# Where the right-hand score units of a sequence block stand in the step loop of a fused attention, LayerNorm and FFN kernel

## The chip, the cores and the metric

The kernel runs on the 8 cores of one Trainium2 chip. Every core computes two of the sixteen sequences with the same program, and no core waits for another. The metric is the device time of the slowest core in microseconds (us).

## The reference

```python
def attn(x):                                  # x: (16, 2048, 1024)
    q = (x @ Wq + bq); k = (x @ Wk + bk); v = (x @ Wv + bv)   # 16 query heads of 64, 2 kv heads
    # position s sees the 256 positions s-128 .. s+127 (keys and values padded with zeros)
    scores = jnp.einsum('bgrsd,bgswd->bgrsw', qg, k_win)
    probs = jax.nn.softmax(scores, axis=-1)
    out = jnp.einsum('bgrsw,bgswd->bgrsd', probs, v_win)
    return out @ Wo + bo
x = layernorm(x + attn(x))
x = layernorm(x + ffn(x))                     # ffn: complex 512 x 512 linear map, W from two small factors
```

## The kernel before, in words

The two sequences of a core are worked through one after the other (variable b). A sequence has 16 blocks of 128 positions. `emit_qkv(b, q)` loads four blocks of x, casts them to bf16 (ACT, L371), transposes them (PE, L381) and makes the queries QT, the keys KT and the values VB of a group of four blocks. Groups 0 and 1 are made ahead of the step loop, groups 2 and 3 at the end of steps 5 and 9.

The step loop has 18 steps k. Step k works on three blocks at once: S = k (scores), P = k-1 (attention, output projection, first LayerNorm) and Q2 = k-2 (FFN, second LayerNorm). The units are:

- `sc_unit(b, S, c, pair)`: two score matmuls (L509) of block S against key block S-1+c, c = 0, 1, 2, into two of the three PSUM banks pSC. The banks go round, (2u)%3 and (2u+1)%3 for the unit with the running number u, so the first matmul of a unit needs the second exp of the unit two before it, and the second matmul needs the first exp of the unit just before it.
- `exp_unit`: the two exps of that unit on ACT (L527), from pSC to EX. The first waits until both matmuls of the unit are done. `mask_unit`: the two masks on GpSimd (POOL, L541) for c = 0 (maskl) and c = 2 (maskr).
- `av_unit(b, P, quad)`, quad = 0 to 3: twelve matmuls (L564) of the masked EX tiles of all three c with VB into pAV[quad % 2]. It waits until that bank has been read by `normts_unit` of quad - 2. `recip_unit` (L582) and `normts_unit` (L592, four instructions) on DVE read the bank.
- `attnT_unit`: eight transposes (L614) and a copy on DVE (L622). `wo_unit`: nine matmuls for each half of the output projection (L639, L643) into pW[0] and pW[1]. `ln1_unit` on DVE: two adds (L682), the sum of squares (L652, tile scr) and four small steps. `rstd1_unit` on ACT: L699 and L704, which wait for the last small step. `x1norm_unit` on DVE (L717).
- `x1t_unit`: eight transposes (L737) and a copy (L744). `ffn_unit`: nine matmuls for each half (L766, L770) into pW[0] and pW[1]. `ln2out_unit`: two adds (L785), which free pW, the same sum of squares (L652), L798 and L803 on ACT, L811 on DVE and the store of y from POOL's queue (L819).

There is no scheduler. Each engine runs its instructions in the order in which the units are called, and a wait on a semaphore holds up everything behind it on its engine. Across engines the order is free but for those waits.

```python
            banks = ((2 * u) % 3, (2 * u + 1) % 3)
                    E.wait(E.res(f"pSC{banks[gq]}")["f"])
                E.wait(E.res(f"avb{quad % 2}")["f"])
                E.wait(E.ev[f"var1_{ring}"])
```

Of the kernel before, what the change touches and what calls it, by code (L numbers as in the profile page):

```python
# [18 lines left out]
def build_nc(debug=False):  # L19
# [138 lines left out]
    def schedule(E):  # L158
# [374 lines left out]
        def mask_unit(b, S, c, pair):  # L533
            m = maskl if c == 0 else maskr
            for gq in range(2):
                quad = pair * 2 + gq
                exi = (S % 2) * 12 + c * 4 + quad
                ev_e = E.ev[f"exp_{S % 2}_{c}_{quad}"]
                if cur == "g":
                    E.wait(ev_e)  # L540
                i = gps.tensor_mul(EX[:, exi * 512:(exi + 1) * 512],  # L541
                                   EX[:, exi * 512:(exi + 1) * 512], m[:]) \
                    if cur == "g" else None
                E.ev[f"msk_{S % 2}_{c}_{quad}"] = E.inc("g", i)

        def av_unit(b, S, quad):
            g = quad % 2
            bank = quad % 2
            vready = E.res(f"VB{S // 4}")["r"]
            vnext = E.res(f"VB{min(S // 4 + 1, 3)}")["r"]  # L550
            if cur == "t":
                E.wait(E.res(f"avb{quad % 2}")["f"])
                E.wait(vready)
                E.wait(vnext)
                for c in range(3):
                    key = ("msk" if c != 1 else "exp") + f"_{S % 2}_{c}_{quad}"
                    E.wait(E.ev[key])
            first = True
            i = None
            for c in range(3):  # L560
                kb = S - 1 + c
                exi = (S % 2) * 12 + c * 4 + quad
                for hh in range(4):
                    i = ten.matmul(  # L564
                        pAV[bank][:, hh * 65:(hh + 1) * 65],
                        EX[:, exi * 512 + hh * 128: exi * 512 + (hh + 1) * 128],
                        VB[:, (kb + 1) * 130 + g * 65: (kb + 1) * 130 + (g + 1) * 65],
                        start=first, stop=(c == 2 and hh == 3)) if cur == "t" else None
                    first = False
            ev = E.inc("t", i if cur == "t" else None)  # L570
            E.ev[f"av_{S % 2}_{quad}"] = ev
            for c in range(3):
                E.res(f"exfree{(S % 2) * 12 + c * 4 + quad}")["f"] = ev

        def recip_unit(b, S, quad):
            ring = S % 2
            i = None
            if cur == "v":
                E.wait(E.ev[f"av_{S % 2}_{quad}"])
                if quad == 0:  # L580
                    E.wait(E.res(f"attn{ring}")["f"])
                i = vec.reciprocal(Rrec[:, ring * 16 + quad * 4: ring * 16 + (quad + 1) * 4],  # L582
                                   ap3(pAV[quad % 2], 64, [[512, 128], [65, 4]]))
            E.inc("v", i)
# [252 lines left out]
        for b in range(NB):  # L837
            if b > 0:
                E.res("KTfree")["f"] = E.ev["lastAV"]["f"]
                E.res("VBfree")["f"] = E.ev["lastAV"]["f"]  # L840
            emit_qkv(b, 0)
            emit_qkv(b, 1)
            if b == 0:
                emit_wbuild()
            if debug and b == 0:
                if cur == "g":
                    gps.wait_ge(SEMH["s"], E.res("QT1")["r"][1])
                    gps.dma_start(dbg["dqt"], QT[:]).then_inc(SEMH["dc"], 16)
                E.c["dc"] += 16
            for k in range(18):  # L850
                S, P, Q2 = k, k - 1, k - 2
                if S < 16:
                    sc_unit(b, S, 0, 0)
                    exp_unit(b, S, 0, 0)
                if 0 <= P < 16:
                    av_unit(b, P, 0)
                if S < 16:
                    sc_unit(b, S, 0, 1)
                    exp_unit(b, S, 0, 1)
                    mask_unit(b, S, 0, 0)  # L860
                    mask_unit(b, S, 0, 1)
                if 0 <= P < 16:
                    av_unit(b, P, 1)
                if 0 <= Q2 < 16:
                    x1t_unit(b, Q2)
                    ffn_unit(b, Q2, 0)
                if 0 <= P < 16:
                    recip_unit(b, P, 0)
                    recip_unit(b, P, 1)
                    normts_unit(b, P, 0)  # L870
                    normts_unit(b, P, 1)
                if S < 16:
                    sc_unit(b, S, 1, 0)
                    exp_unit(b, S, 1, 0)
                if 0 <= P < 16:
                    av_unit(b, P, 2)
                if 0 <= Q2 < 16:
                    ffn_unit(b, Q2, 1)
                if S < 16:
                    sc_unit(b, S, 1, 1)  # L880
                    exp_unit(b, S, 1, 1)
                if 0 <= P < 16:
                    av_unit(b, P, 3)
                    recip_unit(b, P, 2)
                    recip_unit(b, P, 3)
                    normts_unit(b, P, 2)
                    normts_unit(b, P, 3)
                    attnT_unit(b, P)
                if S < 16:
                    sc_unit(b, S, 2, 0)  # L890
                    exp_unit(b, S, 2, 0)
                    mask_unit(b, S, 2, 0)
                if 0 <= Q2 < 16:
                    ln2out_unit(b, Q2)
                if 0 <= P < 16:
                    wo_unit(b, P, 0)
                if S < 16:
                    sc_unit(b, S, 2, 1)
                    exp_unit(b, S, 2, 1)
                    mask_unit(b, S, 2, 1)  # L900
                if 0 <= P < 16:
                    wo_unit(b, P, 1)
                    ln1_unit(b, P)
                    rstd1_unit(b, P)
                    x1norm_unit(b, P)
                if k == 5:
                    emit_qkv(b, 2)
                if k == 9:
                    emit_qkv(b, 3)
                if debug and b == 0 and k == 9:  # L910
                    if cur == "g":
                        gps.wait_ge(SEMH["s"], E.res("KT3")["r"][1])
                        gps.wait_ge(SEMH["v"], E.res("VB3")["r"][1])
                        gps.dma_start(dbg["dkt"], KT[:]).then_inc(SEMH["dc"], 16)
                        gps.dma_start(dbg["dvb"], VB[:]).then_inc(SEMH["dc"], 16)
                    E.c["dc"] += 32
            E.ev["lastAV"] = {"f": ("t", E.c["t"])}
# [88 lines left out]
```

## Time and profile before

| what | us |
|---|---|
| device time, median of 2 runs (1401.92 and 1407.13) | 1404.53 |
| the profiled execution | 1403.19 |
| its span, on the slowest core (4) | 1401.6 |
| spans of the eight cores | 1388.2 to 1401.6 |

The span runs from the first to the last instruction of a core. All durations in this text are from the profiled execution on core 4. The lines L... are those of the kernel before; the functions that the steps call stand above the changed lines and have the same numbers in both kernels.

### The profile page before, as it was taken

The numbers are of one execution on the slowest core, as the hardware profiler recorded it, in microseconds if no ns is written. First come the engines' busy times: TensorE is split into PE (matmuls) and PEld (weight loads), VectorE is DVE, ScalarE is ACT, GpSimd is POOL, SyncE is SP. The second block draws the span as 40 slices with busy tenths as digits, with TensorE's granted clock in tenths as the row PEclk, the third lists the DMA queues.
The fourth block names the chain that finished last, engine by engine and source line by source line (L and its number), as shares of the span: only waits on it lengthen the run. The fifth ranks groups of instructions, "written<-read, shape, count | busy, mean of one in ns | idle before, by whom it ended". The sixth has DMA issues, their size and how long they took to land.

```text
span 1401.6 us, 17008 instructions; the slowest of 8 cores (1388.2 to 1401.6 us)
## 1 busy us (share of the span) xinstructions
PE 851.1 (61%) x4568; PEld 353.4 (25%) x4568; DVE 534.8 (38%) x1539; ACT 396.3 (28%) x673; POOL 358.2 (26%) x324
## 2 busy tenths in 40 slices
PE   0067334676586666676756576676676658676764
PEld 0033001222232223222222232222232223222221
DVE  0001344354414551445554112445225441555453
ACT  3333113223223223323220234323232323323210
POOL 0000004344213440333430105433223421343310
PEclk9998555677687777777776786777687667777676
DMA  4521000000200001000000300000200020000000
GB/s 131 164 78 31 0 0 0 1 25 21 76 0 16 16 33 59 16 16 16 21 26 15 106 31 1 16 16 16 76 1 31 15 76 1 16 21 26 16 16 30
DMA packets 15869, 44.51 MB, mean 32 GB/s; under 512 B 3091, under 2 KB 5539, under 8 KB 15782
## 3 DMA queue, kind: packets, MB, share of 16 engines
q0 software_dynamic: 9216, 33.56, 6.9%
q1 hardware_dynamic: 6566, 9.87, 2.4%
q8 instruction: 45, 0.74, 0.2%
q14 instruction: 42, 0.34, 0.1%
HBM read 26.65 MB, written 16.78 MB: 31 GB/s over the span
## 4 chain that ended last, share of the span: by engine, by line
PE 54%; DVE 19%; issue 10%; DMA 7%; ACT 6%; DVEq 1%; POOL 1%; SPq 0%; ACTq 0%; POOLq 0%
PE pW L766 12%; PE pW L639 12%; PE pW L411 9%; PE pSC L509 4%; PE pAV L564 4%; DVE scr L652 4%; DMA xs<-x 4%; DVE attn L592 4%; PE pT L737 2%; ACT EX L527 2%; PE pW L770 2%; PE pW L643 2%; DVE pre L785 2%; PE pT L614 2%; DVE pre L682 1%
## 5 line engine op out<-in xcount | busy, mean ns | idle before, releaser
L527 ACT ACTIVATE EX<-pSC,expbias 128x512 bf16<-128x512 f32 x384 | 242.7, 683 | 369.6 <-PE pSC L509 368.5
L541 POOL TENSOR_TENSOR EX<-EX,maskr_s 128x512 bf16<-128x512 bf16 x128 | 172.3, 1370 | 333.8 <-ACT EX L527 333.2
L541 POOL TENSOR_TENSOR EX<-EX,maskl_s 128x512 bf16<-128x512 bf16 x128 | 149.6, 1198 | 377.7 <-ACT EX L527 377.7
L639 PE MATMUL pW<-wo_sb,attnT 128*128 128x512 bf16 x512 | 179.8, 514 | 37.0 <-DVE pre L785 35.7
L509 PE MATMUL pSC<-QT,KT 64*128 64x512 bf16 x384 | 111.9, 474 | 109.6 <-ACT EX L527 108.5
L411 PE MATMUL pW<-XT,wq_sb 128*128 128x512 bf16 x512 | 129.2, 420 | 8.9 <-DVE XT L391 8.9
L381 PE MATMUL pT<-identb,x_tm 128*128 128x128 bf16 x256 | 32.0, 304 | 152.7 <-ACT x_tm L371 138.4
L592 DVE TENSOR_SCALAR attn<-pAV,Rrec 128x64 bf16<-128x64 f32 x512 | 110.2, 277 | 14.3 <-DVE attn L592 0.5
L766 PE MATMUL pW<-wrt,x1T 128*128 128x512 bf16 x256 | 92.5, 499 | 36.7 <-DVE Rrec L582 34.5
L652 DVE SCALAR_TENSOR_TENSOR scr<-pre 128x1024 bf16<-128x1024 f32 x64 | 104.5, 1633 | 6.7
L582 DVE RECIPROCAL Rrec<-pAV 128x4 f32<-128x4 f32 x128 | 19.7, 173 | 197.3 <-PE pAV L564 197.3
L639 PEld LDWEIGHTS pW<-wo_sb,attnT 128*128 128x128 bf16 x512 | 57.0, 121 | 142.2 <-issue 123.8
L564 PE MATMUL pAV<-VB,EX 128*128 128x65 bf16 x1536 | 81.5, 211 | 8.0 <-ACT EX L527 3.2
L564 PEld LDWEIGHTS pAV<-VB,EX 128*128 128x128 bf16 x1536 | 65.6, 109 | 47.2 <-issue 47.2
L471 DVE COPY VB<-pT 128x128 bf16<-128x128 bf16 x32 | 7.3, 229 | 182.7 <-PE pT L465 182.7
L420 ACT ACTIVATE QT<-pW,bq_sb 128x512 bf16<-128x512 f32 x64 | 44.0, 687 | 112.3 <-PE pW L411 112.3
L411 PEld LDWEIGHTS pW<-XT,wq_sb 128*128 128x128 bf16 x512 | 53.8, 106 | 82.4 <-issue 33.8
L391 DVE COPY XT<-pT 128x1024 bf16<-128x1024 bf16 x32 | 22.1, 692 | 137.1 <-PE pT L381 137.1
L614 PE MATMUL pT<-identb,attn 128*128 128x128 bf16 x256 | 23.3, 244 | 80.2 <-DVE attn L592 80.2
L509 PEld LDWEIGHTS pSC<-QT,KT 64*128 64x128 bf16 x384 | 23.9, 96 | 169.0 <-issue 164.4
L381 PEld LDWEIGHTS pT<-identb,x_tm 128*128 128x128 bf16 x256 | 24.5, 137 | 159.9 <-issue 159.9
L682 DVE SCALAR_TENSOR_TENSOR pre<-pW,x_tm 128x512 f32<-128x512 f32 x64 | 44.0, 688 | 51.5 <-PE pW L643 51.5
(81 smaller groups left out, 789.5 us busy)
## 6 DMA issues: line engine op xcount, KB each, us to landing
xs<-x POOLq DMA_DIRECT2D x32, 512.0 KB, 4.6
y<-outst POOLq DMA_DIRECT2D x32, 512.0 KB, 3.0
wstage<-wq SPq DMA_DIRECT2D x4, 512.0 KB, 4.5
xs<-wq SPq DMA_DIRECT2D x4, 512.0 KB, 4.6
wstage<-wo SPq DMA_DIRECT2D x4, 512.0 KB, 4.6
xs<-wo SPq DMA_DIRECT2D x4, 512.0 KB, 4.6
wstage<-wk SPq DMA_DIRECT2D x1, 512.0 KB, 4.7
xs<-wv SPq DMA_DIRECT2D x1, 512.0 KB, 4.8
```

Source lines behind the costliest of these rows:

```text
L381: i = ten.transpose(pT[:, c * 128:(c + 1) * 128], x_tm[:, slot * D + c * 128: slot * D + (c + 1) * 128], identb[:]) if cur == "t" else None
L411: i = ten.matmul(pW[bank][:, :], wq_sb[:, c * 1024 + t * 128: c * 1024 + (t + 1) * 128], rhsXT(c), start=(c == 0), stop=(c == 7)) \
L509: i = ten.matmul(pSC[banks[gq]][:, :], lhsT, rhs, start=True, stop=True, tile_position=(rowbase, 0)) if cur == "t" else None
L527: i = sca.activation(EX[:, exi * 512:(exi + 1) * 512], pSC[banks[gq]][:, :], AF.Exp, bias=expbias[:])
L541: i = gps.tensor_mul(EX[:, exi * 512:(exi + 1) * 512], EX[:, exi * 512:(exi + 1) * 512], m[:]) \
L564: i = ten.matmul(pAV[bank][:, hh * 65:(hh + 1) * 65], EX[:, exi * 512 + hh * 128: exi * 512 + (hh + 1) * 128], VB[:, (kb + 1) * 130 + g * ...
L592: i = vec.tensor_scalar(attn[:, ring * 1024 + quadcol[quad] + hh * 64: ring * 1024 + quadcol[quad] + (hh + 1) * 64], ap3(pAV[bank], hh * 6 ...
L614: i = ten.transpose(pT[:, c * 128:(c + 1) * 128], attn[:, ring * 1024 + c * 128: ring * 1024 + (c + 1) * 128], identb[:]) if cur == "t" el ...
L639: ten.matmul(pW[half][:, :], attnT[:, ring * 1024 + c * 128: ring * 1024 + (c + 1) * 128], wo_sb[:, c * 1024 + half * 512: c * 1024 + (hal ...
L652: lambda: vec.scalar_tensor_tensor(scr[:], pre_getter(), 1.0, pre_getter(), ALU.mult, ALU.mult, accum_out=stt[:, c0 + 2:c0 + 3]),
L682: i = vec.scalar_tensor_tensor(pre1[:, ring * 1024 + half * 512: ring * 1024 + (half + 1) * 512], pW[half][:, :], 1.0, x_tm[:, slot * D + ...
L766: ten.matmul(pW[half][:, :], x1T[:, ring * 1024 + c * 128: ring * 1024 + (c + 1) * 128], wsrc[:, wc * 512:(wc + 1) * 512], start=(c == 0), ...
```

## The change

The two units of the right-hand key block, c = 2, with their exps and masks leave the end of the step of their own block and are called at the very start of the next one. They read the same tiles there (QT, KT, EX), and their masks are still ahead of the `av_unit` calls that read them. In a full step the four score pairs c = 2 of P and c = 0 of S are therefore called one behind the other. `av_unit(b, P, 0)` moves behind the first FFN half, `sc_unit(b, S, 1, 0)` stands between it and `av_unit(b, P, 1)`, the first reciprocals and `normts_unit` calls follow that, and `sc_unit(b, S, 1, 1)` stands ahead of `av_unit(b, P, 2)`. No unit is added or left out, and no wait is added or removed by hand.

```diff
--- before.py
+++ after.py
@@ -849,36 +849,41 @@
                 E.c["dc"] += 16
             for k in range(18):
                 S, P, Q2 = k, k - 1, k - 2
+                if 0 <= P < 16:
+                    sc_unit(b, P, 2, 0)
+                    exp_unit(b, P, 2, 0)
+                    mask_unit(b, P, 2, 0)
+                    sc_unit(b, P, 2, 1)
+                    exp_unit(b, P, 2, 1)
+                    mask_unit(b, P, 2, 1)
                 if S < 16:
                     sc_unit(b, S, 0, 0)
                     exp_unit(b, S, 0, 0)
-                if 0 <= P < 16:
-                    av_unit(b, P, 0)
-                if S < 16:
                     sc_unit(b, S, 0, 1)
                     exp_unit(b, S, 0, 1)
                     mask_unit(b, S, 0, 0)
                     mask_unit(b, S, 0, 1)
-                if 0 <= P < 16:
-                    av_unit(b, P, 1)
                 if 0 <= Q2 < 16:
                     x1t_unit(b, Q2)
                     ffn_unit(b, Q2, 0)
                 if 0 <= P < 16:
+                    av_unit(b, P, 0)
+                if S < 16:
+                    sc_unit(b, S, 1, 0)
+                    exp_unit(b, S, 1, 0)
+                if 0 <= P < 16:
+                    av_unit(b, P, 1)
                     recip_unit(b, P, 0)
                     recip_unit(b, P, 1)
                     normts_unit(b, P, 0)
                     normts_unit(b, P, 1)
                 if S < 16:
-                    sc_unit(b, S, 1, 0)
-                    exp_unit(b, S, 1, 0)
+                    sc_unit(b, S, 1, 1)
+                    exp_unit(b, S, 1, 1)
                 if 0 <= P < 16:
                     av_unit(b, P, 2)
                 if 0 <= Q2 < 16:
                     ffn_unit(b, Q2, 1)
-                if S < 16:
-                    sc_unit(b, S, 1, 1)
-                    exp_unit(b, S, 1, 1)
                 if 0 <= P < 16:
                     av_unit(b, P, 3)
                     recip_unit(b, P, 2)
@@ -886,19 +891,10 @@
                     normts_unit(b, P, 2)
                     normts_unit(b, P, 3)
                     attnT_unit(b, P)
-                if S < 16:
-                    sc_unit(b, S, 2, 0)
-                    exp_unit(b, S, 2, 0)
-                    mask_unit(b, S, 2, 0)
                 if 0 <= Q2 < 16:
                     ln2out_unit(b, Q2)
                 if 0 <= P < 16:
                     wo_unit(b, P, 0)
-                if S < 16:
-                    sc_unit(b, S, 2, 1)
-                    exp_unit(b, S, 2, 1)
-                    mask_unit(b, S, 2, 1)
-                if 0 <= P < 16:
                     wo_unit(b, P, 1)
                     ln1_unit(b, P)
                     rstd1_unit(b, P)
```

PE in step 6, which is the first after group 2 of `emit_qkv`. Before, from the step's start to the second FFN half (L509 score pairs, L564 attention times values, L737 transposes, L766 and L770 FFN):

```order
L509 MATMUL pSC<-QT,KT 128x512 x2
L564 MATMUL pAV<-VB,EX 128x65 x12
L509 MATMUL pSC<-QT,KT 128x512 x2
L564 MATMUL pAV<-VB,EX 128x65 x12
L737 MATMUL pT<-identb,x_tm 128x128 x8
L766 MATMUL pW<-wrt,x1T 128x512 x4
L766 MATMUL pW<-witn,x1T 128x512 x4
L770 MATMUL pW<-beta_row,ones_row 128x512
L509 MATMUL pSC<-QT,KT 128x512 x2
L564 MATMUL pAV<-VB,EX 128x65 x12
L766 MATMUL pW<-wit,x1T 128x512 x4
L766 MATMUL pW<-wrt,x1T 128x512 x4
```

The same engine and place in the changed kernel:

```order
L509 MATMUL pSC<-QT,KT 128x512 x8
L737 MATMUL pT<-identb,x_tm 128x128 x8
L766 MATMUL pW<-wrt,x1T 128x512 x4
L766 MATMUL pW<-witn,x1T 128x512 x4
L770 MATMUL pW<-beta_row,ones_row 128x512
L564 MATMUL pAV<-VB,EX 128x65 x12
L509 MATMUL pSC<-QT,KT 128x512 x2
L564 MATMUL pAV<-VB,EX 128x65 x12
L509 MATMUL pSC<-QT,KT 128x512 x2
L564 MATMUL pAV<-VB,EX 128x65 x12
L766 MATMUL pW<-wit,x1T 128x512 x4
L766 MATMUL pW<-wrt,x1T 128x512 x4
```

Two score pairs separated by an attention group have become four pairs (eight matmuls) in a row, and the two attention groups of the start now stand behind the first FFN half.

ACT from the first exp of that step into the next one. Before (L527 exp, L798 and L803 the second LayerNorm, L699 and L704 the first):

```order
L527 ACTIVATE EX<-pSC,expbias 128x512 x10
L798 ACTIVATE st<-st 128x1
L803 ACTIVATE rstd<-st,neghalf 128x1
L527 ACTIVATE EX<-pSC,expbias 128x512 x2
L699 ACTIVATE st<-st 128x1
L704 ACTIVATE rstd<-st,neghalf 128x1
L527 ACTIVATE EX<-pSC,expbias 128x512 x10
```

In the changed kernel:

```order
L527 ACTIVATE EX<-pSC,expbias 128x512 x12
L798 ACTIVATE st<-st 128x1
L803 ACTIVATE rstd<-st,neghalf 128x1
L699 ACTIVATE st<-st 128x1
L704 ACTIVATE rstd<-st,neghalf 128x1
L527 ACTIVATE EX<-pSC,expbias 128x512 x12
L798 ACTIVATE st<-st 128x1
```

The two exps between the two LayerNorms have gone, and all twelve exps of a step stand together, behind the first LayerNorm's two instructions.

POOL around the loads of group 2 at the end of step 5. Before (L541 masks, L819 store of y, L363 loads of x):

```order
L541 TENSOR_TENSOR EX<-EX,maskl_s 128x512 x4
L541 TENSOR_TENSOR EX<-EX,maskr_s 128x512 x2
L819 DMA y<-outst 128x1024
L541 TENSOR_TENSOR EX<-EX,maskr_s 128x512 x2
L363 DMA xs<-x 128x1024 x4
L541 TENSOR_TENSOR EX<-EX,maskl_s 128x512 x4
```

In the changed kernel:

```order
L541 TENSOR_TENSOR EX<-EX,maskr_s 128x512 x4
L541 TENSOR_TENSOR EX<-EX,maskl_s 128x512 x4
L819 DMA y<-outst 128x1024
L363 DMA xs<-x 128x1024 x4
L541 TENSOR_TENSOR EX<-EX,maskr_s 128x512 x4
```

The last masks of the step stood between the store and the loads; now they stand behind the loads.

## Rows read from the trace of the kernel before

**Rows 1.** The page: its span and PE's busy time.

```profile
span 1401.6 us, 17008 instructions; the slowest of 8 cores (1388.2 to 1401.6 us)
...
PE 851.1 (61%) x4568; PEld 353.4 (25%) x4568; DVE 534.8 (38%) x1539; ACT 396.3 (28%) x673; POOL 358.2 (26%) x324
```

**Rows 2.** The page: chain that ended last, by engine.

```profile
PE 54%; DVE 19%; issue 10%; DMA 7%; ACT 6%; DVEq 1%; POOL 1%; SPq 0%; ACTq 0%; POOLq 0%
```

**Rows 3.** Windows: length; busy us (instructions) of PE, PEld, DVE, ACT, POOL; clock; DMA.

```profile
616.10:643.66 27.56, 18.89 (x113) 7.61 (x112) 13.99 (x44) 8.48 (x16) 10.35 (x10) 0.75 0.03 13
229.70:238.80 9.10, 6.83 (x15) 1.24 (x14) 5.46 (x4) 7.18 (x12) 7.56 (x5) 0.50 0.00 0
```

**Rows 4.** Timeline, start of step 13: start us, us, instruction, [idle before].

```profile
643.67 0.39 PE L509 MATMUL pSC<-QT,KT 64*128 64x512 bf16 x2
...
644.72 1.78 DVE L652 SCALAR_TENSOR_TENSOR scr<-pre 128x1024 bf16<-128x1024 f32 x1
...
648.21 1.25 ACT L527 ACTIVATE EX<-pSC,expbias 128x512 bf16<-128x512 f32 x2
...
649.02 0.58 PE L509 MATMUL pSC<-QT,KT 64*128 64x512 bf16 x1 [4.17 <-ACT EX L527]
...
650.33 1.04 PE L737 MATMUL pT<-identb,x_tm 128*128 128x128 bf16 x8
...
652.49 0.58 PE L766 MATMUL pW<-wrt,x1T 128*128 128x512 bf16 x1 [1.12 <-DVE Rrec L582]
```

**Rows 5.** Timeline, rest of step 12.

```profile
628.31 0.39 PE L509 MATMUL pSC<-QT,KT 64*128 64x512 bf16 x2
...
628.63 0.54 PE L564 MATMUL pAV<-VB,EX 128*128 128x65 bf16 x12
...
631.47 0.54 PE L564 MATMUL pAV<-VB,EX 128*128 128x65 bf16 x12
...
632.40 1.83 DVE L592 TENSOR_SCALAR attn<-pAV,Rrec 128x64 bf16<-128x64 f32 x8
...
634.49 0.68 PE L614 MATMUL pT<-identb,attn 128*128 128x128 bf16 x8 [2.48 <-DVE attn L592]
...
636.79 3.57 PE L639 MATMUL pW<-wo_sb,attnT 128*128 128x512 bf16 x8 [1.08 <-DVE pre L785]
...
640.83 0.61 PE L509 MATMUL pSC<-QT,KT 64*128 64x512 bf16 x2
...
641.37 2.05 PE L639 MATMUL pW<-wo_sb,attnT 128*128 128x512 bf16 x8
```

**Rows 6.** Timeline, TensorE in step 0, score pairs alone.

```profile
232.75 1.16 PE L509 MATMUL pSC<-QT,KT 64*128 64x512 bf16 x2 [0.35 <-ACT EX L527]
234.26 1.16 PE L509 MATMUL pSC<-QT,KT 64*128 64x512 bf16 x2 [0.35 <-ACT EX L527]
```

**Rows 7.** Windows, tile scr alone, at the ends of 14 steps.

```profile
257.70:263.00 5.30, 1.23 (x2) 0.98 0.00 0
...
343.00:347.90 4.90, 1.32 (x2) 1.00 0.18 70
...
sum 78.30, DVE 27.57; mean DVE 1.97
```

**Rows 8.** Timeline, end of step 5 and loads of group 2.

```profile
369.95 2.27 POOL L541 TENSOR_TENSOR EX<-EX,maskr_s 128x512 bf16<-128x512 bf16 x2
...
372.15 1.13 POOL L363 DMA_DIRECT2D xs<-x  x2
...
374.81 0.29 ACT L704 ACTIVATE rstd<-st,neghalf 128x1 f32<-128x1 f32 x1
...
377.20 1.04 ACT L371 CAST x_tm<-xs 128x1024 bf16<-128x1024 f32 x1 [2.10 <-DMA xs<-x]
```

**Rows 9.** Timeline, start of step 6.

```profile
411.41 0.53 PE L509 MATMUL pSC<-QT,KT 64*128 64x512 bf16 x2 [0.23 <-issue]
...
414.28 1.04 PE L737 MATMUL pT<-identb,x_tm 128*128 128x128 bf16 x8
```

## The prediction

> **What bounds the kernel now.** I read the page first. The span is 1401.6 us and no engine fills it: TensorE (PE) is busy for 851.1 us, ACT for 396.3 us [rows 1]. The chain that ended last puts 54% on PE, 19% on DVE, 10% on gaps between dependent instructions, 6% on ACT [rows 2]. So the bound is a chain that goes from engine to engine inside each step; a step gets longer where PE comes to a wait with nothing queued in front of it.
>
> The windows view gives one step: step 12 takes 27.56 us, in which PE is busy for 18.89, DVE for 13.99, ACT for 8.48 and POOL for 10.35, at a mean granted clock of 0.75 [rows 3]. ACT and POOL have room; the matter is when their work comes.
>
> Then the timeline. PE's waits in a full step are four. (a) At the start: the second matmul of the second score pair waits 4.17 us for the first exp [rows 4]. ACT has just finished the previous step's first LayerNorm, and behind PE's last output-projection matmul that takes long: the step begins at 643.67, DVE starts the sum of squares at 644.72 (1.05 later), it takes 1.78, the exp starts 1.71 after its end (648.21), the matmul 0.81 after that (649.02). (b) 1.12 us ahead of the first FFN half at 652.49, behind the transposes at 650.33. (c) 2.48 us ahead of the transposes at 634.49, from the eight normalisations. (d) 1.08 us ahead of the output projection at 636.79 [rows 5]. The change touches (a), adds a wait between (b) and (c), and takes filling out of (d).
>
> **The change, part by part.** A "full step" is one of steps 2 to 15 of both sequences, 28 in all; 24 begin behind another step's LayerNorm, 4 (steps 6 and 10) begin behind group 2 or 3 of the QKV part, when ACT is already free.
>
> 1. Start of a step, four score pairs in a row. With three PSUM banks a pair's second matmul needs the first exp of the pair before it. Before, the wait for the first exp came in the second pair; it still does, and only the attention group that stood in it (hidden there) is gone. But now two more pairs follow that ACT paces. What that costs is shown by step 0, where the pairs stand alone: they start 1.51 us apart, 232.75 and 234.26 [rows 6]. Before, from the matmul at 649.02 to the transposes at 650.33 it was 1.31 us [rows 4], one matmul and one attention group. Now it is 2 x 1.51 + 0.55 for the last matmul at 1.2 GHz = 3.57, so +2.26. Nothing hides it: the transposes need L717, which was done in time for them at 650.33 [rows 4], but they stand behind the scores in PE's order. Bounds: ACT cannot take less than the 1.25 us of two exps [rows 4] per pair, so at least 2.5 + 0.4 - 1.31 = +1.6.
>
> 2. The masks leave the sum of squares. Two masks used to run on POOL at the step's end. The sum of squares took 1.97 us on average in 14 windows there, but 1.23 where no mask and no store ran beside it, and 1.32 in one with a store (DMA share 0.18) [rows 7]. Now no mask is called between the centre of one step and the next first exp, so I take 1.28: -0.69 in wait (a). Bounds: -0.74 and 0. The masks' new place costs nothing: the four that the moved attention groups need take 2 x 2.27 us [rows 8] behind the first exp, and ahead of the first of those groups stand three more pairs, the transposes and nine FFN matmuls, some 10 us.
>
> 3. The new wait in the middle. `av_unit(P, 2)` reuses the PSUM bank of `av_unit(P, 0)` and waits for its normalisation, which on DVE stands behind the reciprocal of quad 1. Before, both groups were over long before the first FFN half ended, and from the end of that half (628.31) to the last attention group (631.47) it was 3.16 us [rows 5]. Now, counted from the same point: attention group 0.35 (an estimate, between a pair's 0.32 from 628.31 to 628.63 and the group's own 0.54), score pair 0.32, second attention group starts at 0.67. Normalisation starts 0.93 after a group's start (631.47 to 632.40), its first four of eight take half of 1.83, and PE reacts 0.26 after the end (634.23 to 634.49) [rows 5]: the third group starts at 0.67 + 0.93 + 0.92 + 0.26 = 2.78. From there to the last group it was 2.84 with a pair of 0.32 in it, so 2.52: 5.30. That is +2.1. Of it some 0.7 is the two groups that were free at the start of the step, and 1.4 is waiting, net of the pairs. The last group, the reciprocal, and wait (c) follow as before. Bounds: +0.7 if the wait vanished, +2.6 if everything there ran at 1.2 GHz.
>
> 4. End of a step. The pair ahead of the second output-projection half cost 0.54 (640.83 to 641.37) [rows 5] and is gone: -0.5. The pair behind the transposes stood in wait (d), which DVE's add ends, so it gives nothing. Bounds: -0.54 and 0.
>
> 5. Loads of groups 2 and 3, 4 times. The two masks (2.27 us) stood on POOL ahead of the x loads; the first cast on ACT started at 377.20, 2.1 after LayerNorm at 375.1, waiting for the DMA [rows 8]. Without the masks the loads are issued 2.2 earlier, and LayerNorm ends 0.4 earlier: -2.2 each. Bounds: -2.6 and 0.
>
> Sum. 24 steps x (2.26 - 0.69 + 2.1 - 0.5 = 3.17) = +76. Four steps behind QKV: before, from the first pair to the transposes 2.87 us (411.41 to 414.28) [rows 9]; now 3 x 1.51 + 0.55 = 5.08, +2.2, and with 2.1 - 0.5 that is +3.8 each, +15. Loads: 4 x -2.2 = -9. Step 16 of each sequence has no pairs of its own but the new middle: +2.1 and -0.4, about +4 for two. Steps 0 and 1: two pairs leave the ACT-paced step 0 (-3.0), are back in front of step 1's attention, whose own waits then overlap less: 0 with 2 us either way. Total +86. The profiled execution was 1403.2, the median of the runs 1.3 above it: 1403.2 + 86 + 1.3 = about 1490 us.
>
> The bounds of the terms: lowest per step 1.6 - 0.74 + 0.7 - 0.54 = +1.0, highest 2.26 + 2.6 = +4.9; over 28 steps +28 and +137, with the other terms 1425 and 1542.
>
> **Rivals.**
>
> A. The clock stays low through the middle. Behind waits (c) and (d) the first half of the output projection ran at 1.2 GHz, 3.57 us for eight matmuls, and only the second, right behind it, mostly at 2.4 GHz, 2.05 [rows 5]. If the new breaks in the middle keep it from rising, the second FFN half takes the 3.57 of the slow kind in place of about 2: +1.7 and more x 28 = +50, 1540 us. For it: in step 0, where pairs wait for ACT, the clock was 0.50 throughout [rows 3]. Against it: ahead of the new wait PE has run nine dense FFN matmuls, and the breaks are about a microsecond. The Trainium skill (TensorE: Matmul & The Clock Gate, section "A second HAM failure mode: psum-queue depth-cycling") describes this: a kernel that cycles PSUM banks and idles briefly between groups swings between the two clocks. That rule speaks against the change; no row here shows it for breaks this short.
>
> B. The other side: the scores raise the clock. Eight matmuls now stand where there was one long idle; if they bring the clock to 2.4 GHz ahead of the transposes, the pairs go at 1.3 (-0.4), and the transposes and the first FFN half lose half their time (about -2.1). Together -2.5 x 28 = -70: 1420 us, which is within 2%. It decides if the clock is up when the first FFN half starts. Against it: the 0.50 of step 0, seven such pairs long [rows 3, 6].
>
> C. As B, and the output projection's first half is fast too (-1.7 x 28): 1372 us. Waits (c) and (d) stand ahead of it as before, so little speaks for it.
>
> **How the numbers follow.** Forecast 0.78, A 0.12, B 0.08, C 0.02. The forecast case alone spans about 1455 to 1525; to leave out no more than 2 in 10 I take 1450 to 1528. About 2%, 28 us, is what a measurement of this kernel can tell from no change: forecast and A are slower by more (0.90), B is within it (0.08), C is faster (0.02).
>
> **What would show it.** Right: in a full step four score pairs 1.5 us apart behind the first exp; the transposes L737 some 8.4 us behind the step's start (it was 6.66 in step 13 [rows 4]); a new wait of PE for L592 of about a microsecond ahead of the third attention group; L652 at the step's end at 1.2 to 1.35 us; masks in runs of eight; the first x load right behind the store. PE's busy time hardly changes and its waits grow by about 86 us, two thirds of it in waits for ACT's exps and the rest for DVE's normalisations. Wrong: L766 of the first half at half its time (B) or of the second at twice (A), or no wait ahead of the third group.

## The result and the profile after

The changed kernel takes 1568.04 us (median of 11 runs), the kernel before 1401.98 us (10 runs): the ratio is 1.119 with a 95% interval of 1.117 to 1.121. The forecast was 1490, with 1450 to 1528 as its range. The direction was right; the slowdown, 166 us, is nearly twice the 86 us that were forecast.

The page after, its span and PE's busy time, answers to [rows 1], and the chain that ended last, by engine, to [rows 2]:

```profile
span 1568.5 us, 16950 instructions; the slowest of 8 cores (1559.8 to 1568.5 us)
...
PE 931.1 (59%) x4506; PEld 370.1 (24%) x4568; DVE 510.3 (33%) x1539; ACT 396.2 (25%) x673; POOL 328.0 (21%) x324
...
PE 49%; DVE 16%; issue 12%; ACT 11%; DMA 7%; POOL 2%; DVEq 1%; ACTq 1%; SPq 0%; POOLq 0%
```

The span grew by 166.9 us, and PE's busy time by 80 us although PE has the same work. An equal list of matmuls can only be busier if it runs slower. The trace after lacks 62 of its matmul records (x4506 for x4568), 60 of them in the FFN halves, so PE was busy for somewhat more than 931.1 us. DVE is busy for 24.5 us less and ACT for the same time; ACT's share of the chain went from 6% to 11%.

The windows view of step 12, three stretches of it: the whole step, then from the end of the first FFN half to the start of the second, then the second half. The columns are those of [rows 3]:

```profile
666.93:701.03 34.10, 22.00 (x112) 8.44 (x114) 13.54 (x44) 8.48 (x16) 9.70 (x9) 0.70 0.04 16
681.60:685.36 3.76, 2.52 (x41) 1.64 (x41) 2.08 (x10) 2.53 (x4) 0.00 (x0) 0.95 0.02 4
685.36:689.15 3.79, 3.57 (x13) 1.14 (x11) 0.18 (x1) 0.00 (x0) 0.00 (x0) 0.56 0.00 0
```

The second FFN half of the same step before the change:

```profile
629.01:631.14 2.13, 2.13 (x15) 0.77 (x11) 0.18 (x1) 1.11 (x2) 0.00 (x0) 1.00 0.00 0
```

A full step is 34.1 us now. In the middle stretch the clock is up (0.95, the 2.4 GHz level but for its first moments), and in the second FFN half right behind it, nine matmuls in a row, it is 0.56: mostly 1.2 GHz. Before the change it was 1.00 there. In 22 of the 24 full steps of the table below it is now 0.52 to 0.60 in the second half. In the other two, with breaks of 0.93 and 0.94 us ahead of the third attention group, it stayed at 1.00. The timeline of PE in the same step, with one DVE row, answers to [rows 4, 5]:

```profile
671.73 1.16 PE L509 MATMUL pSC<-QT,KT 64*128 64x512 bf16 x2 [4.19 <-ACT EX L527]
...
673.29 1.16 PE L509 MATMUL pSC<-QT,KT 64*128 64x512 bf16 x2 [0.40 <-ACT EX L527]
...
674.86 0.58 PE L509 MATMUL pSC<-QT,KT 64*128 64x512 bf16 x1 [0.41 <-ACT EX L527]
...
675.37 1.04 PE L737 MATMUL pT<-identb,x_tm 128*128 128x128 bf16 x8
...
681.60 0.64 PE L564 MATMUL pAV<-VB,EX 128*128 128x65 bf16 x12
...
683.44 1.83 DVE L592 TENSOR_SCALAR attn<-pAV,Rrec 128x64 bf16<-128x64 f32 x8
...
684.97 0.58 PE L564 MATMUL pAV<-VB,EX 128*128 128x65 bf16 x12 [1.04 <-ACT EX L527]
...
687.05 1.85 PE L766 MATMUL pW<-wrt,x1T 128*128 128x512 bf16 x4
...
692.17 1.01 PE L614 MATMUL pT<-identb,attn 128*128 128x128 bf16 x8 [2.48 <-DVE attn L592]
...
694.81 3.57 PE L639 MATMUL pW<-wo_sb,attnT 128*128 128x512 bf16 x8 [1.62 <-DVE pre L785]
```

At the start of the step (666.93) PE's wait for the first exp ends at 671.73, 4.80 later, and the pairs follow 1.56 apart; the transposes stand 8.44 behind the start, where the forecast had 8.4. The first FFN half ends at 681.60. PE then starts the third attention group only at 684.97, after a wait of 1.04. The column names an exp of ACT for it, but this group reads exps of the step before and of this step's start, which had long ended. What it waits for is its PSUM bank, which the first half of DVE's normalisation (begun at 683.44) frees at about 684.3; DVE's order alone moves this wait in the run on the shorter break below. The four matmuls at 687.05 take 1.85; the same four took 1.03 before:

```profile
629.87 1.03 PE L766 MATMUL pW<-wrt,x1T 128*128 128x512 bf16 x4
```

The tile scr alone, the sum of squares, answers to [rows 7] (shortest, median and longest in ns, then the first and last start in us):

```profile
L652 DVE SCALAR_TENSOR_TENSOR scr<-pre x64: 1225/1226/1226, 258.2 to 1555.4; 128x1024 bf16<-128x1024 f32 x64
```

It is 1.23 us in all 64 cases. The masks did stretch it, and they are gone from there. The loads of group 2, answering to [rows 8]:

```profile
390.58 0.60 POOL L819 DMA_DIRECT2D y<-outst  x1 [16.98 <-DVE outst L811]
...
391.17 1.06 POOL L363 DMA_DIRECT2D xs<-x  x2
...
394.88 0.29 ACT L704 ACTIVATE rstd<-st,neghalf 128x1 f32<-128x1 f32 x1
...
398.00 1.04 ACT L371 CAST x_tm<-xs 128x1024 bf16<-128x1024 f32 x1 [2.82 <-DMA xs<-x]
```

The loads leave right behind the store (L819), ahead of LayerNorm's end, but the cast that waits for the first one starts 6.83 us after the loads' issue, where it took 5.05. Over the four groups made inside the loop it took 6.83, 5.51, 5.84 and 5.23 us, and before the change 5.05, 4.95, 5.05 and 4.11.

Averaged over the full steps of each kernel (24, those behind another step's LayerNorm), from PE's timeline. A stretch ends where PE's next one starts:

| stretch of a full step, us | before | after | difference | forecast |
|---|---|---|---|---|
| start, to the FFN's transposes | 6.82 | 8.48 | +1.66 | +1.57 |
| transposes and first FFN half | 6.10 | 6.22 | +0.12 | 0 |
| first FFN half's end to the second's start | 0.86 | 3.86 | +3.00 | |
| second FFN half | 2.17 | 3.59 | +1.42 | |
| its end to the transposes of the attention output | 3.38 | 3.04 | -0.34 | |
| (these three, the middle) | 6.41 | 10.49 | +4.08 | +2.1 |
| end of the step | 9.11 | 8.76 | -0.35 | -0.5 |
| sum | 28.44 | 33.96 | +5.52 | +3.17 |

24 full steps make +132 of the 167 us, the four steps behind the QKV parts +26 (30.84 against 24.31 us each), the last step of each sequence +7.5 for both, the four waits for the loads -3 in all, and the QKV parts, steps 0, 1 and 17 what is left, about +4.

### The profile page after: what moved, and what is told of

Same layout as the page of the kernel before. It is cut to its first block, busy times and chain, and to the rows that moved or that the text cites. A ratio compares the mean times of both kernels' runs of the same rounds, so it can differ in the third digit from the quotient of the medians.

```text
span 1568.5 us, 16950 instructions; the slowest of 8 cores (1559.8 to 1568.5 us)
## 1 busy us (share of the span) xinstructions
PE 931.1 (59%) x4506; PEld 370.1 (24%) x4568; DVE 510.3 (33%) x1539; ACT 396.2 (25%) x673; POOL 328.0 (21%) x324
## 4 chain that ended last, share of the span: by engine, by line
PE 49%; DVE 16%; issue 12%; ACT 11%; DMA 7%; POOL 2%; DVEq 1%; ACTq 1%; SPq 0%; POOLq 0%
PE pW L766 12%; PE pW L639 10%; PE pW L411 8%; ACT EX L527 8%; PE pSC L509 4%; DMA xs<-x 4%; DVE attn L592 4%; PE pAV L564 4%; DVE scr L652 3%; PE pT L614 2%; POOL EX L541 2%; PE pW L770 2%; DVE pre L785 2%; PE pW L643 2%; DMA xs<-wq 1%
## 5 line engine op out<-in xcount | busy, mean ns | idle before, releaser
L527 ACT ACTIVATE EX<-pSC,expbias 128x512 bf16<-128x512 f32 x384 | 242.6, 682 | 224.9 <-PE pSC L509 222.1
L509 PE MATMUL pSC<-QT,KT 64*128 64x512 bf16 x384 | 154.2, 478 | 147.8 <-ACT EX L527 146.2
L541 POOL TENSOR_TENSOR EX<-EX,maskr_s 128x512 bf16<-128x512 bf16 x128 | 147.6, 1178 | 292.2 <-ACT EX L527 292.2
L541 POOL TENSOR_TENSOR EX<-EX,maskl_s 128x512 bf16<-128x512 bf16 x128 | 145.1, 1160 | 157.2 <-ACT EX L527 157.2
L819 POOL DMA_DIRECT2D y<-outst x32 | 19.0, 595 | 615.1 <-DVE outst L811 615.1
L766 PE MATMUL pW<-wrt,x1T 128*128 128x512 bf16 x224 | 102.8, 601 | 48.7 <-POOL EX L541 30.1
L798 ACT ACTIVATE st<-st 128x1 f32<-128x1 f32 x32 | 6.5, 203 | 411.9 <-DVE st L662 411.9
L564 PE MATMUL pAV<-VB,EX 128*128 128x65 bf16 x1536 | 76.4, 205 | 36.3 <-ACT EX L527 29.8
L509 PEld LDWEIGHTS pSC<-QT,KT 64*128 64x128 bf16 x384 | 30.0, 96 | 247.4 <-issue 243.6
L652 DVE SCALAR_TENSOR_TENSOR scr<-pre 128x1024 bf16<-128x1024 f32 x64 | 78.4, 1226 | 6.7
L564 PEld LDWEIGHTS pAV<-VB,EX 128*128 128x128 bf16 x1536 | 61.1, 104 | 73.7 <-issue 73.7
L614 PE MATMUL pT<-identb,attn 128*128 128x128 bf16 x256 | 30.5, 293 | 79.9 <-DVE attn L592 79.9
L744 DVE COPY x1T<-pT 128x1024 bf16<-128x1024 bf16 x32 | 22.1, 692 | 140.5 <-PE pT L737 140.5
```

The lines of the kernel that those rows point to most:

```text
L509: i = ten.matmul(pSC[banks[gq]][:, :], lhsT, rhs, start=True, stop=True, tile_position=(rowbase, 0)) if cur == "t" else None
L527: i = sca.activation(EX[:, exi * 512:(exi + 1) * 512], pSC[banks[gq]][:, :], AF.Exp, bias=expbias[:])
L541: i = gps.tensor_mul(EX[:, exi * 512:(exi + 1) * 512], EX[:, exi * 512:(exi + 1) * 512], m[:]) \
L564: i = ten.matmul(pAV[bank][:, hh * 65:(hh + 1) * 65], EX[:, exi * 512 + hh * 128: exi * 512 + (hh + 1) * 128], VB[:, (kb + 1) * 130 + g * ...
L614: i = ten.transpose(pT[:, c * 128:(c + 1) * 128], attn[:, ring * 1024 + c * 128: ring * 1024 + (c + 1) * 128], identb[:]) if cur == "t" el ...
L652: lambda: vec.scalar_tensor_tensor(scr[:], pre_getter(), 1.0, pre_getter(), ALU.mult, ALU.mult, accum_out=stt[:, c0 + 2:c0 + 3]),
```

## The experiments

Two theories of the middle. M: the third attention group waits for its bank, PE idles, the clock falls in that break, and the second FFN half pays for it. H: the clock is low there because of the score pairs that ACT paces at the start of the step. The first two kernels undo one half of the change each. M expects the second FFN half slow in the first and fast in the second, H the other way round.

**Only the middle.** Against the changed kernel:

```diff
-sc/exp/mask_unit(b, P, 2, 0); sc/exp/mask_unit(b, P, 2, 1)      # start of the step
+sc/exp/mask_unit(b, S, 2, 0)                                    # behind attnT_unit, as before
+sc/exp/mask_unit(b, S, 2, 1)                                    # ahead of wo_unit(b, P, 1), as before
```

> Only the middle is changed: both c = 2 units stay at the end of their own step, so a step starts with two score pairs, and the attention groups stand in and behind the first FFN half as in the changed kernel. Theory M (the break before the third attention group, which waits for its bank, lets the clock fall, and the second FFN half then runs at 1.2 GHz): the second FFN half takes about 3.7 us as in the changed kernel, the step is 28.3 + 4.1 (middle) - 0.7 (second attention group gone from the start), some 31.8 us, total about 1500 us. Rival H (the clock is low there because of the score pairs that ACT paces at the start of the step): the second FFN half takes 2.15 us, the step about 30.2, total about 1455 us.

Measured: 1519.57 us, ratio 1.083 (1.081 to 1.086), 20 us above M's number. The second FFN half takes 3.65 us on average in the full steps. With two score pairs at the start, as in the kernel before, it is as slow as with four, which speaks against H. But it does not show M's way to the low clock either. The windows view of one step, from the end of the first FFN half to the start of the second, then the second half:

```profile
633.17:638.04 4.87, 3.58 (x41) 2.33 (x41) 2.09 (x10) 2.53 (x4) 0.00 (x0) 0.50 0.00 0
638.04:641.98 3.94, 3.94 (x13) 1.14 (x11) 0.18 (x1) 0.00 (x0) 0.00 (x0) 0.52 0.02 4
```

In 13 of the 24 full steps the clock was 0.50 ahead of the break already, as here: it did not fall in the break, it never rose. What kept it down there is not shown. The full steps are also longer ahead of the second half, 4.34 us on average against 3.86 in the changed kernel, which is part of the 20 us.

**Only the start.** Against the changed kernel:

```diff
 sc_unit(b, S, 0, 1); exp_unit(b, S, 0, 1); masks
+av_unit(b, P, 0); av_unit(b, P, 1)
 x1t_unit(b, Q2); ffn_unit(b, Q2, 0)
-av_unit(b, P, 0); sc/exp_unit(b, S, 1, 0); av_unit(b, P, 1)
 recips and normts of quads 0 and 1
+sc/exp_unit(b, S, 1, 0)
-sc/exp_unit(b, S, 1, 1); av_unit(b, P, 2); ffn_unit(b, Q2, 1)
+av_unit(b, P, 2); ffn_unit(b, Q2, 1); sc/exp_unit(b, S, 1, 1)
```

> Only the start is changed: four score pairs in a row, but the first two attention groups right behind them and ahead of the FFN's transposes, and the middle as before the change. Theory M: no wait for an attention bank, the second FFN half at 2.15 us, start of the step about 2.2 us longer than before, step about 30.2 us, total about 1455 us. Rival H: the second FFN half at 3.7 us, step about 31.8, total about 1500 us.

Measured: 1480.71 us, ratio 1.055 (1.053 to 1.058). The second FFN half is at 2.20 us, as M says, with four score pairs at the start: H falls here. The total missed by 26 us: the start of the step is 10.0 us, 3.2 over the kernel before and not 2.2, since both attention groups now run there at 1.2 GHz and in PE's way. The two halves of the change cost 117 and 79 us alone against 166 together.

**The same pieces, a shorter break.** Against the changed kernel:

```diff
 av_unit(b, P, 0)
+recip_unit(b, P, 0); normts_unit(b, P, 0)
 sc_unit(b, S, 1, 0); exp_unit(b, S, 1, 0)
 av_unit(b, P, 1)
-recip_unit(b, P, 0); recip_unit(b, P, 1); normts_unit(b, P, 0); normts_unit(b, P, 1)
+recip_unit(b, P, 1); normts_unit(b, P, 1)
```

> The changed kernel with the reciprocal and the normalisation of quad 0 called right behind its attention group, ahead of those of quad 1, so that the bank of the third group comes free about 0.9 us earlier. Theory M: the break shrinks from 1.0 us to some tenths, the clock stays at 2.4 GHz, the second FFN half takes 2.15 us; step 34.1 - 1.0 - 1.6 = 31.5, total about 1495 us. Rival H: only the break goes, step 33.1, total about 1540 us.

Measured: 1477.4 us, ratio 1.054 (1.052 to 1.056). PE's order is that of the changed kernel, instruction for instruction; only DVE's order differs. Its timeline around the third group:

```profile
650.36 0.54 PE L564 MATMUL pAV<-VB,EX 128*128 128x65 bf16 x12
...
652.96 0.52 PE L564 MATMUL pAV<-VB,EX 128*128 128x65 bf16 x12 [0.37 <-ACT EX L527]
653.32 1.02 PE L766 MATMUL pW<-wit,x1T 128*128 128x512 bf16 x4
654.18 1.03 PE L766 MATMUL pW<-wrt,x1T 128*128 128x512 bf16 x4
```

The break ahead of the group is 0.37 in place of 1.04 us (0.34 and 1.06 on average), and the four matmuls take 1.02 and 1.03 in place of 1.85. Per full step 3.1 us are gone, 0.9 as the shorter break, 1.45 in the second FFN half, and the rest in the transposes and the output projection behind it (8.1 us in place of 8.8). This last part M's number did not have, and the total came out 18 us below it.

**The second FFN half ahead of the third group.** Against the changed kernel:

```diff
 sc_unit(b, S, 1, 1); exp_unit(b, S, 1, 1)
-av_unit(b, P, 2)
 ffn_unit(b, Q2, 1)
+av_unit(b, P, 2)
 av_unit(b, P, 3)
```

> The changed kernel with the second FFN half ahead of the third attention group, so that PE has nine matmuls to run while DVE normalises quad 0. Theory M: no break in the middle, the second FFN half at 2.15 us, the last attention group starts about 3.4 us earlier; step about 31 us, total about 1480 us, near the 1490 us of the forecast. Rival H: the second FFN half at 3.7 us, step about 32.5, total about 1525 us.

Measured: 1473.77 us, ratio 1.051 (1.049 to 1.053); the second FFN half at 2.15 us, the step at 30.78.

**Idle time alone.** The two kernels above also take the wait away. This one leaves the wait on DVE where it is and gives PE something to do ahead of it:

```diff
 sc_unit(b, S, 1, 1); exp_unit(b, S, 1, 1)
+five times: matmul(pW[1], x1T[:, 0:128 of the ring], wit[:, 0:512], start=True, stop=True)
 av_unit(b, P, 2)
```

> The changed kernel with five extra 128x512 matmuls on PE in the middle break, right ahead of the third attention group; they write pW[1], which the second FFN half starts afresh, so the output is the same and no wait is taken away. They add about 1.1 us of PE work where PE idled for about 1.0. Theory M in its narrow form (PE's own idle time there makes the clock fall): the second FFN half goes back to 2.15 us, the step from 34.1 to about 32.6, total about 1525 us, faster than the changed kernel although it has more work. Rival (the clock falls for what the small attention matmuls do, or for the wait on DVE as such): the second FFN half stays at 3.7 us and the total at 1568 us or above.

Measured: 1518.84 us, ratio 1.082 (1.079 to 1.086); 49 us faster than the changed kernel with 5 matmuls more in each step that has an FFN part. The windows view, from the end of the first FFN half to the second's start, then the second half:

```profile
665.11:669.23 4.12, 3.92 (x46) 2.18 (x46) 2.08 (x10) 2.51 (x4) 0.00 (x0) 0.85 0.00 0
669.23:671.37 2.14, 2.14 (x15) 0.78 (x12) 0.18 (x1) 0.02 (x1) 0.00 (x0) 1.00 0.00 0
```

And its timeline:

```profile
667.76 1.25 PE L785 MATMUL pW<-wit,x1T 128*128 128x512 bf16 x5
668.87 0.52 PE L564 MATMUL pAV<-VB,EX 128*128 128x65 bf16 x12
669.23 1.03 PE L766 MATMUL pW<-wit,x1T 128*128 128x512 bf16 x4
670.10 1.03 PE L766 MATMUL pW<-wrt,x1T 128*128 128x512 bf16 x4
```

The filler (L785 is its line in that kernel) ends as the group may start. The stretch to the second half is as long as before (4.12 us here, 3.89 on average against 3.86), so nothing was gained there; the clock is at 1.00 in the second half, 2.14 us. So the fall of the clock comes from PE's own idling in the break and not from what it waits for. The Trainium skill (TensorE: Matmul & The Clock Gate, section "A second HAM failure mode: psum-queue depth-cycling") describes such swings where PE idles briefly between groups while it cycles PSUM banks; the trace agrees, with breaks of 0.2 and 1.04 us in 22 of 24 steps of the changed kernel.

**Terms 2 and 5 alone, on the kernel before.** 

```diff
 mask_unit(b, S, 0, 0)
+mask_unit(b, P, 2, 1)
 mask_unit(b, S, 0, 1)
 ...
 sc_unit(b, S, 2, 1); exp_unit(b, S, 2, 1)
-mask_unit(b, S, 2, 1)
```

> The kernel before with one call moved: the two masks of the last score pair of a block stand one step later, between the masks of the next block's first and second pair, so that on POOL they run behind the LayerNorm's sum of squares and behind the x loads. This is terms 2 and 5 of the prediction alone. If they are right: the sum of squares 1.25 to 1.35 us in place of 1.97 on average, 0.7 us less per step in 24 steps, 2 us less at each of the 4 loads: about 1376 us. Rival (the sum of squares is stretched by the store of y, not by the masks): no change in it, total 1395 to 1402 us.

Measured: 1375.26 us, ratio 0.980 (0.978 to 0.982): 27.6 us faster, about what terms 2 and 5 add up to. The start of a full step is 6.15 in place of 6.82 us, which is term 2. The agreement of the sum is in part luck: the loads gave some 4 us and not 9, and the rest came from other stretches of the step, above all the transposes and the first FFN half (5.88 in place of 6.10 us).

**The order on ACT.** On the kernel before:

```diff
 sc/exp_unit(b, S, 0, 0); av_unit(b, P, 0); sc/exp_unit(b, S, 0, 1)
+if k - 1 not in (5, 9) and k < 17: rstd1_unit(b, Q2); x1norm_unit(b, Q2)
 ...
 ln1_unit(b, P)
-rstd1_unit(b, P); x1norm_unit(b, P)
+if k in (5, 9, 16): rstd1_unit(b, P); x1norm_unit(b, P)
```

> The kernel before with the two ACT instructions of the first LayerNorm and its DVE normalisation called one step later, behind the first four exps of the step (not ahead of the QKV parts). If the wait at the start of a step is due to ACT's order alone, PE goes on at once and waits instead for the normalisation ahead of the FFN's transposes: start of the step 6.8 to about 5.9 us, total about 1382 us. Rival: the first masks now fall on the sum of squares and stretch it, and the gain is eaten, 1395 to 1410 us.

Measured: 1467.93 us, ratio 1.047 (1.042 to 1.053), slower than either expectation. The rival named the cause and not its size. The timeline of DVE and POOL:

```profile
634.88 2.27 POOL L541 TENSOR_TENSOR EX<-EX,maskr_s 128x512 bf16<-128x512 bf16 x2
...
635.64 7.00 DVE L652 SCALAR_TENSOR_TENSOR scr<-pre 128x1024 bf16<-128x1024 f32 x1
...
637.10 4.46 POOL L541 TENSOR_TENSOR EX<-EX,maskl_s 128x512 bf16<-128x512 bf16 x4
...
643.86 0.20 ACT L699 ACTIVATE st<-st 128x1 f32<-128x1 f32 x1 [6.10 <-DVE st L662]
```

One sum of squares of 7.00 us: it began while the first of six masks ran back to back on POOL (634.88 to 641.56), and ended 1.08 us after the last of them. In the kernel before, the one at 644.72 [rows 4] ended likewise, at 646.50, 1.09 us after the two masks that ran ahead of it:

```profile
643.14 2.27 POOL L541 TENSOR_TENSOR EX<-EX,maskr_s 128x512 bf16<-128x512 bf16 x2
```

The start of the step is 9.63 us on average; 18 of the 64 sums of squares took 5.98 to 7.34 us. The Trainium skill (SBUF — State Buffer, section "SBUF: two separate sides") says that a GpSimd instruction and a DVE instruction with two SBUF inputs hold their shared port pair exclusively for an instruction; the trace agrees that they exclude each other, and shows more: here DVE did not get in between two masks of a run. It is no general rule. In the kernel before, the sum of squares of the second LayerNorm begins at 637.36 while the first of two masks runs, and ends after 1.57 us; it is the second mask that waits, and the two take 3.24 us in place of 2.27:

```profile
636.70 3.24 POOL L541 TENSOR_TENSOR EX<-EX,maskr_s 128x512 bf16<-128x512 bf16 x2 [11.00 <-ACT EX L527]
...
637.36 1.57 DVE L652 SCALAR_TENSOR_TENSOR scr<-pre 128x1024 bf16<-128x1024 f32 x1
```

What decides who goes first is not shown.

**The second FFN half last.** On the kernel before:

```diff
 av_unit(b, P, 2)
-ffn_unit(b, Q2, 1)
 sc_unit(b, S, 1, 1); exp_unit(b, S, 1, 1)
 av_unit(b, P, 3)
+ffn_unit(b, Q2, 1)
 recips and normts of quads 2 and 3; attnT_unit(b, P)
```

> The kernel before with the second FFN half behind the last attention group, so that DVE's normalisation of quads 2 and 3 runs beside it. The wait of 2.5 us ahead of the transposes shrinks to about 0.5: 2.0 us per step, 28 steps, about 1346 us. If the clock also stays at 2.4 GHz through the transposes and the first half of the output projection, 1.7 us more per step: about 1300 us.

Measured: 1354.43 us, ratio 0.966 (0.964 to 0.968). The wait of 2.5 us ahead of the transposes is 0.4. The clock was also up in the transposes (0.61 us on average, 0.71 before) and in the first half of the output projection in part of the steps (2.65 us on average from its first matmul to its last, 3.44 before). Part of both was given back: the start of a step grew from 6.82 to 7.94 us, with sums of squares up to 3.2 us. So the total is near the first expectation by a gain of the second and a loss that neither had.

**Both moves that helped.**

> The two moves that helped alone, together: the last two masks of a block behind the next block's first masks, and the second FFN half behind the last attention group. In the run with the FFN half moved alone the start of a step had grown from 6.8 to 7.8 us, its sums of squares ran up to 3.2 us beside the masks; if that is the masks, the start falls to about 6.15 as in the run with the masks moved alone: 26.96 - 1.65 = 25.3 us per step in 24 steps, 2 us less at 4 loads: 1354 - 40 - 8 = about 1306 us. Rival (the start grew for the earlier transposes, not for the masks): about 1346 us, the loads alone.

Measured: 1309.68 us, ratio 0.936 (0.933 to 0.939). The start is 6.71 us, some way back from 7.94, and the first half of the output projection 1.91 us on average, 1.82 at a clock of 1.00 in 22 of the 24 full steps. The clock is not up everywhere ahead of it: in 8 of the 24 the second FFN half has 0.63 to 0.67, with no break of more than 0.23 us between the two halves. So a break is not the only thing that goes with a low clock there.

**And ACT's order, with POOL held back.** As the last one with the order of ACT of the kernel above, and

```diff
 rstd1_unit(b, Q2); x1norm_unit(b, Q2)
+on POOL: E.wait(E.ev[f"var1_{Q2 % 2}"])
 mask_unit(b, S, 0, 0)
```

> As the run before, and the first LayerNorm's two ACT instructions and its normalisation one step later behind the first four exps, but with POOL waiting for the LayerNorm's variance ahead of the step's first mask, so that no mask can run beside the sum of squares. In the earlier run without that wait the sum of squares took up to 7.3 us. If those masks were the whole reason for its 1468 us, the start of a step is now bounded by the normalisation: 1.05 + 1.23 + 1.2 + 0.5 + 0.3 + 0.8 + 0.25 = about 5.3 us in place of 6.15: 0.85 us x 24 less than the run before, about 1285 us. If something else made it slow: 1306 us or more.

Measured: 1284.76 us, ratio 0.918 (0.915 to 0.920). Its page:

```profile
span 1279.7 us, 17040 instructions; the slowest of 8 cores (1273.8 to 1279.7 us)
...
PE 779.4 (61%) x4568; PEld 337.6 (26%) x4568; DVE 515.1 (40%) x1539; ACT 396.0 (31%) x673; POOL 363.9 (28%) x324
```

And its tile scr:

```profile
L652 DVE SCALAR_TENSOR_TENSOR scr<-pre x64: 1224/1226/1522, 256.1 to 1266.6; 128x1024 bf16<-128x1024 f32 x64
```

The same move of ACT's two instructions that cost 65 us alone gives 25 us once no mask can run beside the first LayerNorm's sum of squares; the longest, 1.52 us, are of the second LayerNorm. The total is the expected one, in part by luck: the start of a step was to fall by 0.85 us to 5.3 and fell by 0.5, from 6.71 to 6.20; the other half of the gain of 1.0 us a step came behind it. This version is 8% faster than the kernel before and 18% faster than the changed one.

## Why the prediction was wrong

Wrong was the size of term 3, the new wait in the middle, and with it the choice between the forecast and rival A. The new waits of PE were nearly right; what the forecast left out is the clock behind them.

- Start of a step (terms 1 and 2): right. The wait for the first exp ended 4.80 us behind the step's start, the pairs were 1.56 apart where 1.51 was taken, the sum of squares 1.23 for 1.28; +1.66 measured, +1.57 forecast. The masks-late run shows term 2 by itself.
- Middle (term 3): +4.08 for +2.1. The step that failed is "from there to the last group it was 2.84": the price of the second FFN half was taken from a row in which the clock was up, while the same term put a break of about a microsecond ahead of it. It measured 3.59 in place of 2.17 us: 1.42 us of the difference. The upper bound of the term has the same fault: it was +2.6 "if everything there ran at 1.2 GHz", while rival A priced the second half alone at +1.7 more, and the middle measured +4.08. Rival A had this cost, by a clock that the breaks keep from rising, where in the changed kernel it rose and fell again. It was given 0.12 on the ground that nine dense matmuls stand ahead of the break and that the break is short. Dense work ahead did bring the clock up (0.95 in that stretch) and did not keep it up through the break. That the break does it is shown by the short-break, the reordered and the filler kernels, all with the second half at 2.14 to 2.15 us.
- Also in term 3, the third group started 3.37 us after the first FFN half's end in step 12, not 2.78. 0.23 of that is the first group and the pair at the end of the slow stretch (the second group starts at 0.90 for 0.67), and 0.35 is that it starts 1.53 us after the normalisation does, where half of it and PE's reaction made 1.18. The last 0.35 us need not belong to the wait for DVE: in the short-break kernel the first half of the normalisation was over at 652.22 and the group started at 652.96, 0.74 later, and before the change a group whose bank was free followed 0.68 behind a score matmul that had waited (649.02 to 649.70). What takes this time is not shown.
- End of a step (term 4): -0.35 for -0.5; the transposes of the attention output now run at 1.2 GHz (1.01 for 0.68 us), again behind the slow half.
- Steps behind the QKV parts: +6.5 for +3.8, of the same middle.
- Loads (term 5): -3 for -9. They did leave earlier, but from issue to cast it took 5.2 to 6.8 us in place of 4.1 to 5.05. Why is not shown. That they stood right behind a store does not settle it: in the kernel before, a load issued 0.53 us behind a store (775.86, ahead of the second sequence) had its cast start 5.24 us later, hardly more than 5.05. In the masks-late run too, 24 of the 27.6 us are the full steps (27.45 for 28.44 each), so the loads can have given some 4 us there: -9 was too much in both kernels.
- Rival A's 1540 us was too low by 28 us, since it took the rest of the forecast as it was, with the third group's start, the transposes and the loads. Rivals B and C did not occur: the clock stayed at 1.2 GHz through the ACT-paced pairs (1.16 for two matmuls, as in step 0 before).

The signs were announced: a wait for the normalisation ahead of the third group, L652 at 1.23, masks in runs of eight and PE's waits for ACT were all there. "PE's busy time hardly changes" was wrong, and its growth by 80 us is the mark of the clock. The time in which PE was not busy grew by 87 us, where 86 was said; the match is closer than the reasoning, since the missing matmul records count as idle there and the terms for the middle and the loads were off.

## What to carry to other kernels

When an order puts a wait on PE ahead of a dense run of matmuls, price that run at the lower clock too, and give the case as much weight as the higher one: here a break of about a microsecond was followed by a slow second FFN half in 22 of 24 steps, which makes 1.4 us a step on average. Move independent dense work into a bank-reuse wait, or shorten it by letting the consumer's engine free the first bank first (91 us here, from DVE's order alone). A DVE instruction like the sum of squares here, when it is on the critical chain, wants GpSimd held back by a wait, not only usually idle. Each such move has to be tried together with what it releases, because the same move cost 65 us in one surrounding and gave 25 us in another.

## What the runs showed of the hardware that had not been expected

- A break of 1.04 us (and one of 0.2) in a stretch of small matmuls at 2.4 GHz went ahead of a clock of 0.56 in the next 3.79 us, and likewise in 22 of 24 steps; with a break of 0.37 it stayed up, and with five filler matmuls in the break it stayed up too and the kernel became 49 us faster. It is no sharp rule: in the two other steps the clock stayed up behind breaks of 0.93 and 0.94, and in the middle-only run it was low ahead of the break in 13 of 24 steps.
- A DVE sum of squares of 1.23 us lasted 7.00 us beside six masks run back to back on GpSimd; in the changed kernel, with no mask beside it, all 64 took 1.225 to 1.226 us. Between two masks of a pair it did get in, in the kernel before, and then the second mask was the one to wait.
- The first of the 512 KB loads of a group, issued 0.6 us behind a 512 KB store in place of 2.8, was ready for its cast after 5.2 to 6.8 us in place of 4.1 to 5.05. The cause is open.
